# fp16 row sums for steps 13 and 14, their low parts' place on VectorE, and a different wait ahead of the experts' first layers

## The chip, the cores and the metric

The kernel runs on one core of one Trainium2 chip. The metric is the device time of one execution in microseconds (us). The engines are named as in the profile: PE (TensorE, matmuls), DVE (VectorE), ACT (ScalarE), POOL (GpSimd), SP (the queue that issues most DMAs).

## What is computed

Two batches of 512 tokens of width 128 and a context of 154 rows per batch. Layer normalisation, cross attention with 16 heads of width 64, a residual, layer normalisation again, and a mixture of 8 experts of which each token takes its best 2, with a residual:

```python
lat = layer_norm(_layernorm(x), g_l, b_l)            # 512 queries
kv_input = concatenate([layer_norm(ctx, g_m, b_m), lat])   # 154 + 512 = 666 keys
dots = einsum('bhid,bhjd->bhij', q, k) * 64 ** -0.5
attn = softmax(dots)
x = x + (einsum('bhij,bhjd->bhid', attn, v) merged) @ Wout
probs = softmax(n @ Wg); top 2, scaled to sum 1      # n = _layernorm(x)
h = relu((n masked) @ W1[e] + b1[e]); y = h @ W2[e] + b2[e]
x = x + sum over e of y * score[e]
```

## The kernel before, in words

**Attention.** It runs in STEPS = 16 steps `s`; a step is one pair of heads of one batch. In a step the 666 keys come in KT = 6 tiles of 111. Per tile PE computes the scores of both heads, keys on partitions and queries along the row (`dots`, L448 to 472; the shift by the row maxima is one of its matmuls, L470), ACT takes the exponential into `probs` (`exponent`, L785 to 792), and POOL adds the tiles of probabilities up in `psum_acc[:, s % 2]`, five additions a step (`gather`, L1330 to 1344, semaphore `added`). Between the tiles PE makes the scores of the next step for the maxima (`lead_next`), which DVE reduces (`reduce_max`, `join_max`), PE turns (`turn_max`) and DVE spreads into `max_row` (`spread_max`, L1005); the next step's `dots` need it. At the end of a step PE multiplies the probabilities with V (`pv`, L474 to 486).

**The sum of a row.** The softmax denominator is the sum of psum_acc over its 111 partitions, made on PE with a matrix of ones (`total`, L488 to 501). Up to step 12 (`s < HALVED`, HALVED = STEPS - 3 = 13) psum_acc is first split into two fp16 parts: ACT makes `acc_hi` (`sum_high`, L798 to 802), DVE makes `acc_lo`, the difference (`sum_low`, L1018 to 1021), and PE multiplies both (L493). From step 13 on PE multiplies psum_acc itself in fp32 (L499). ACT copies the sum to `recips` (`copy_sum`, L804), DVE takes reciprocals in four pieces (`reciprocal`, L1023), and POOL multiplies the step's output with them (`normalise`, L1346 to 1350, semaphore `o_norm`). acc_hi and acc_lo exist once, psum_acc and recips twice.

**The order of work** is written out by hand, one queue for each engine, with semaphores between them. In step s, `total(s - 1)` is queued on PE ahead of the last tile of `pv` (SUM_AT = 5), for s = 14 ahead of the first. ACT has `sum_high(s - 1)` behind the exponentials of step s, DVE has `sum_low(s - 1)` behind that step's spread maxima, and the reciprocals of step s - 2 behind that. Step 14 makes no projections of a later step; PE multiplies the output of batch 0 with Wout instead (`out_project(0)`).

**From step 15 on.** The attention output of batch 0 becomes x1 (`x1_and_moments(0)`), is normalised (`rstd_x1(0)` on POOL, `norm_x1(0)` on DVE), turned on PE (`turn_x2(0)`) and split into a high and a low part (`split_x2(0)`, three instructions). DVE's queue there: x1, norm, reciprocals of step 12, split, reciprocals of step 13, the gate (`gate_start`, `gate_end`), reciprocals of step 14. POOL's queue: `rstd_x1(0)`, `normalise(12)`, three running sums of step 15, `normalise(13)`, two more, `w2_low(1)`, then the experts. PE's queue: `turn_x2(0)`, the six tiles of `dots(15)`, `logits(0)`, `total(14)`, the six of `pv(15)`, `layer_one(0)`, `turn_scores(0)`, `layer_one(1)`, `total(15)`, `bias_term(0)`, `layer_one(2)` and so on. SP writes the turned scores to memory and reads them back as broadcast rows (`spread`, one DMA for each expert).

**The experts.** g = 0 to 15 is batch times expert. `layer_one(g)` (L655 to 669) makes two halves of hidden values (c = 0, 1) in four PSUM banks `hid_ps[n % 4]`, n = 2g + c, so expert g overwrites the banks of g - 2. ACT makes relu and its high part; the low part of the first half is made by POOL (`low_first`), that of the second half by DVE (`low_second`, L1156) or, for g in ON_POOL (L55: 5 to 10, 13, 14), by POOL (L1324 to 1328). For g in ON_POOL, ACT writes the second relu to SBUF (`relu_second_ring`), so the high and the low part are read from there; otherwise relu stays in the bank. The wait of `layer_one` for c = 1 is `second_low(pe, g - 2)` (L288 to 293): the low part of g - 2 must be made. `layer_two(g)`, queued LAG = 2 experts later, multiplies with W2; `add_expert` on DVE weighs and adds, each needing its broadcast rows. For g >= SCALED = 13 the weight goes into the hidden values ahead of relu (`scale_hidden`, DVE).

Of the kernel before, what the change touches and what calls it, by code (L numbers as in the profile page):

```python
# [27 lines left out]
STEPS = PAIRS * B  # L28
# [17 lines left out]
VH = KT // 2  # L46
RC = 4
WB = 4
HALVED = STEPS - 3
SUM_AT = KT - 1  # L50
W1_AT = {2: 0, 3: 1, 8: 2, 9: 3, 10: 4, 11: 5, 12: 6, 13: 7}
W2_HI_AT = {11: (0,), 12: (1, 2), 13: (3, 4), 14: (5, 6, 7)}
# [2 lines left out]
ON_POOL = [5, 6, 7, 8, 9, 10, 13, 14]  # L55
# [29 lines left out]
def xattn_moe(nc, x, ctx_in, g_m, b_m, g_l, b_l, wq, wkv, wout, wg, w1, b1, w2, b2, out):  # L85
    with ExitStack() as stack:
# [168 lines left out]
        r1_done = sem("r1_done")  # L255
# [132 lines left out]
        def _(pe):  # L388
# [99 lines left out]
            def total(s, bank=pj):  # L488
                if s < HALVED:
                    pe.wait_ge(acc_lo_done, s + 1)  # L490
                    for part in (acc_hi, acc_lo):
                        for h in range(2):
                            mm = pe.matmul(bank[h * HD:(h + 1) * HD, :], ones_h[0:KP, :], part[0:KP, h, :],  # L493
                                           start=(part is acc_hi), stop=(part is acc_lo))
                    mm.then_inc(sum_ready, 1)
                    return
                pe.wait_ge(added, (KT - 1) * (s + 1))
                for h in range(2):
                    mm = pe.matmul(bank[h * HD:(h + 1) * HD, :], ones[0:KP, :], psum_acc[0:KP, s % 2, h, :],  # L499
                                   start=True, stop=True)  # L500
                mm.then_inc(sum_ready, 1)
# [76 lines left out]
            for s in range(STEPS - 1):  # L578
                made = s + 2 < STEPS
                ahead = 0 if s else 1  # L580
                for kt in range(ahead):
                    dots(s, kt)
                for kt in range(ahead, KT):
                    dots(s, kt)
                    lead_next(s + 1, kt - ahead)
                if ahead:
                    lead_next(s + 1, KT - 1)
                if made:
                    pe.wait_ge(exp_done, s * KT + KT - 1)
                    if batch_of(s + 2) == 0:  # L590
                        pe.wait_ge(wqk_split, pair_of(s + 2))
                    elif s == 2:
                        pe.wait_ge(kv_lo_pool, 3)
                    project_q(s + 2)
                    project_k(s + 2, 0, sc[:, 0, 1, :])
                    pe.wait_ge(exp_done, s * KT + KT)
                    project_k(s + 2, 1, sc[:, 1, 0, :])
                else:
                    pe.wait_ge(tail_loaded, 16 * 4)
                    pe.wait_ge(max_done, (s + 2) * UNITS - 1)  # L600
                    pe.wait_ge(o_norm, STEPS - 4)
                    out_project(0, x1_ps[0], range(PAIRS))
                if v_half(s):
                    if v_weights(v_half(s)[0]) > 0:
                        pe.wait_ge(wv_split, v_weights(v_half(s)[0]))
                    pe.wait_ge(max_done, (s + 2) * UNITS - 1)
                    project_v(*v_half(s))
                pe.wait_ge(exp_done, s * KT + KT)
                if s == 1:
                    pe.wait_ge(max_done, (s + 2) * UNITS)  # L610
                    for n in range(QT):
                        mm = turn_inputs(1, n, pj[:, n * P:(n + 1) * P])
                    mm.then_inc(norm_turned, 1)
                    for n in range(QT, QT + CT):
                        at = P + (n - QT) * CP
                        mm = turn_inputs(1, n, sc[:, 1, 1, at:at + CP])
                    mm.then_inc(norm_turned, 1)
                turn_max(s + 1)
                if s > HALVED:
                    total(s - 1)  # L620
                for kt in range(KT):
                    if kt == SUM_AT and 1 <= s <= HALVED:
                        if s == 1:
                            pe.wait_ge(kv_ready, 3)
                        total(s - 1)
                    pv(s, kt)
# [28 lines left out]
            def layer_one(g):  # L655
                b, e = g // E, g % E
                if e == 0:
                    pe.wait_ge(x2_lo, b + 1)
                pe.wait_ge(w1_split, min(g + 1, E))
                for c in range(HC):  # L660
                    n = g * HC + c
                    if n < 4:
                        pe.wait_ge(exp_done, STEPS * KT - (1 if n < 2 else 0))
                    elif c == 0:
                        pe.wait_ge(r0_done, g - 1)
                    else:
                        second_low(pe, g - 2)
                    three(hid_ps[:, n % 4, :], w1_hi[:, e, c * P:(c + 1) * P], w1_lo[:, e, c * P:(c + 1) * P],
                          kv_hi[:, b, 0:N], kv_lo[:, b, 0:N]).then_inc(hid_ready, 1)
# [52 lines left out]
            s = STEPS - 1  # L722
# [41 lines left out]
        def _(act):  # L764
# [56 lines left out]
            g = E * HC  # L821
# [31 lines left out]
            def w2_high(e):  # L853
                act.wait_ge(tail_loaded, 16 * 4)
                act.wait_ge(k_lo_done, 2 * (STEPS - WB + e // 2 + 1))
                act.copy(w2_hi(e), w2_raw[:, e * HC:(e + 1) * HC, :]).then_inc(w2_hi_ready, 1)

            for s in range(STEPS):
                if s >= 1:
                    copy_output(s - 1)  # L860
                for kt in range(KT):
                    exponent(s, kt)
                if s + 2 < STEPS:
                    q_high(s + 2)
                    k_high(s + 2, 0, sc[:, 0, 1, :])
                    k_high(s + 2, 1, sc[:, 1, 0, :])
                if 2 <= s <= HALVED:
                    sum_high(s - 1)
                if v_half(s):
                    copy_v(*v_half(s))  # L870
                if s == 1:
                    second_inputs()
                    sum_high(s - 1)
                    second_high()
                if s >= 1:
                    copy_sum(s - 1)
                if s + 1 in W1_AT:
                    w1_high(W1_AT[s + 1])
                for e in W2_HI_AT.get(s, ()):
                    w2_high(e)  # L880

            def gate_exp_of(b):
                act.wait_ge(gate_sub, b + 1)
# [68 lines left out]
        def _(dve):  # L952
# [27 lines left out]
            def k_low(n, half, bank):  # L980
                dve.wait_ge(k_hi_done, 2 * n + half + 1)
                at = k_cols(half)
                dve.tensor_tensor(k_pair[:, n % QKB, 1, at], bank[:, 0:k_width(half)],
                                  k_pair[:, n % QKB, 0, at].bitcast(F32), ALU.subtract).then_inc(k_lo_done, 1)
# [20 lines left out]
            def spread_max(n, bank=sc[:, 1, 1, :]):  # L1005
                dve.wait_ge(neg_turned, n + 1)
                dve.tensor_tensor(max_row[:, n % 2, :].rearrange("p (t c) -> p t c", t=QT),  # L1007
                                  bank[:, 0:P].unsqueeze(1).to_broadcast([P, QT, P]),
                                  sel[:, :].unsqueeze(2).to_broadcast([P, QT, P]), ALU.mult).then_inc(row_done, 1)
# [8 lines left out]
            def sum_low(s):  # L1018
                dve.wait_ge(acc_hi_done, s + 1)
                dve.tensor_tensor(acc_lo[0:KP, :, :], psum_acc[0:KP, s % 2, :, :], acc_hi[0:KP, :, :],  # L1020
                                  ALU.subtract).then_inc(acc_lo_done, 1)
# [27 lines left out]
            g = E * HC  # L1049
# [33 lines left out]
            for s in range(STEPS - 1):  # L1083
                made = s + 2 < STEPS
                for u in range(UNITS):
                    reduce_max(s + 1, u)
                join_max(s + 1)
                if made:
                    q_low(s + 2)
                    k_low(s + 2, 0, sc[:, 0, 1, :])  # L1090
                spread_max(s + 1)
                if made:
                    k_low(s + 2, 1, sc[:, 1, 0, :])
                if s == 0:
                    second_moments()
                if 1 <= s <= HALVED:
                    sum_low(s - 1)
                if 2 <= s <= HALVED:
                    for c in range(RC):
                        reciprocal(s - 2, c)  # L1100

# [9 lines left out]
            def norm_x1(b):  # L1111
                dve.wait_ge(rstd_ready, RSTDS + b + 1)
                apply_norm(b, [(t, acc[:, b, t, :]) for t in range(QT)])
# [80 lines left out]

            x1_and_moments(0, x1_ps[0])
            norm_x1(0)
            for c in range(RC):
                reciprocal(STEPS - 4, c)
            split_x2(0)
# [230 lines left out]
```

## Time and profile before

| | us |
|---|---|
| median of 3 runs (341.89 to 341.97) | 341.89 |
| the profiled execution | 342.18 |
| its span | 340.2 |
| busy in it: PE, DVE, ACT, POOL | 331.9, 272.7, 214.8, 290.3 |
| the granted TensorE clock | full in all 40 slices |

The span runs from the first to the last instruction of the trace; the time around it is 2.0 us. An engine's busy time is an average over the whole: PE is busy nearly always, POOL nearly always during attention. What a part is worth is read from the timeline around it. Times of the timeline are counted from the span's start: attention's steps run from about 20 us at 15.8 us each, step 14 begins at 241 us, step 15 at 262 us, the experts at 276 us.

### The profile page before, as it was taken

What the parts mean: (1) busy time and instruction counts of PE and PEld (TensorE: products, weight loads), DVE (VectorE), ACT (ScalarE), POOL (GpSimd) and SP (SyncE); (2) the same over time, 40 slices, a digit from 0 to 9 for tenths busy, and PEclk for the clock granted to TensorE, in tenths of its full rate; (3) what the DMA queues carried; (4) which work ended last, traced back from release to release, by engine and by line L of the source; (5) the groups of instructions that cost most, each with busy time, mean ns of one, the idle gap of its engine ahead of it and who ended that gap; (6) DMA issues with size and microseconds to landing.
All of it is one profiled execution on the core that took longest, in us unless ns stands there. A gap on an engine that the chain in (4) does not pass through costs nothing.

```text
span 340.2 us, 6018 instructions
## 1 busy us (share of the span) xinstructions
PE 331.9 (98%) x2209; PEld 221.8 (65%) x2209; DVE 272.7 (80%) x413; ACT 214.8 (63%) x305; POOL 290.3 (85%) x188
## 2 busy tenths in 40 slices
PE   7899999999999999999999999999999999999986
PEld 7666666575747565665657584756594548888766
DVE  5989566988989899999898797979737797399494
ACT  2565678584949475675858494957622746487954
POOL 4639999999999999999999999899994899488543
PEclk9999999999999999999999999999999999999999
DMA  4640000000010000000000000000000006100520
GB/s 128 183 129 0 2 0 4 0 17 0 2 31 10 23 2 0 3 1 2 15 2 15 18 0 17 0 2 1 2 0 3 0 0 198 53 2 0 175 106 33
DMA packets 9049, 10.03 MB, mean 29 GB/s; under 512 B 1015, under 2 KB 6061, under 8 KB 9021
## 3 DMA queue, kind: packets, MB, share of 16 engines
q1 hardware_dynamic: 8725, 9.52, 9.0%
q8 instruction: 18, 0.29, 0.3%
q10 hardware_dynamic: 296, 0.13, 0.1%
q14 instruction: 10, 0.08, 0.1%
HBM read 9.09 MB, written 0.56 MB: 28 GB/s over the span
## 4 chain that ended last, share of the span: by engine, by line
PE 93%; issue 2%; ACT 2%; POOL 1%; DVE 1%; POOLq 0%; ACTq 0%; DVEq 0%
PE xo L484 25%; PE sc L464 21%; PE sc L470 6%; PE sc L390 5%; PE sc L391 4%; PE sc L392 4%; PE mx L421 3%; PE xo L421 3%; PE mx L572 2%; PE xo L572 2%; PE xo L493 2%; PE sc L505 2%; PE mx L391 1%; PE mx L390 1%; PE mx L392 1%
## 5 line engine op out<-in xcount | busy, mean ns | idle before, releaser
L1343 POOL TENSOR_TENSOR psum_acc<-psum_acc,probs 111x1024 f32<-111x1024 f32 x64 | 164.0, 2563 | 6.9
L792 ACT ACTIVATE probs<-sc 111x1024 f32<-111x1024 f32 x96 | 98.3, 1028 | 18.5 <-PE sc L470 11.3
L484 PE MATMUL xo<-probs,v_sb 111*64 111x512 f32 x384 | 88.0, 596 | 0.0
L464 PE MATMUL sc<-q_pair,k_pair 64*111 64x512 f32 x576 | 85.9, 401 | 0.8 <-ACT v_sb L782 0.4
L464 PEld LDWEIGHTS sc<-q_pair,k_pair 64*111 64x111 f32 x576 | 44.7, 170 | 28.3 <-issue 11.5
L484 PEld LDWEIGHTS xo<-probs,v_sb 111*64 111x64 f32 x384 | 26.3, 137 | 42.7 <-issue 39.4
L1026 DVE RECIPROCAL recips<-recips 128x128 f32<-128x128 f32 x64 | 54.0, 904 | 0.0
L992 DVE TENSOR_REDUCE part_max<-mx 128x2 f32<-128x888 f32 x32 | 34.7, 1084 | 21.0 <-PE mx L421 19.5
L808 ACT COPY recips<-xo 128x512 f32<-128x512 f32 x16 | 9.4, 587 | 57.5 <-PE xo L493 48.8
L1343 POOL TENSOR_TENSOR psum_acc<-probs 111x1024 f32<-111x1024 f32 x16 | 39.3, 2458 | 7.1 <-ACT probs L792 6.9
L470 PE MATMUL sc<-max_row,ones_r 64*111 64x512 f32 x192 | 38.3, 391 | 0.0
L1321 POOL TENSOR_TENSOR relu_lo<-relu_ring,relu_hi 128x512 fp32r<-128x512 f32 x16 | 20.7, 1291 | 15.7 <-ACT relu_hi L906 14.3
L992 DVE TENSOR_REDUCE part_max<-xo 128x2 f32<-128x888 f32 x30 | 32.5, 1084 | 1.7 <-PE xo L421 0.3
L1350 POOL TENSOR_TENSOR o_t<-o_t,recips 128x512 f32<-128x512 f32 x16 | 20.7, 1294 | 5.2 <-DVE recips L1026 5.2
L1020 DVE TENSOR_TENSOR acc_lo<-psum_acc,acc_hi 111x1024 f16<-111x1024 f32 x13 | 24.0, 1847 | 1.2 <-ACT acc_hi L802 1.2
L470 PEld LDWEIGHTS sc<-max_row,ones_r 64*111 64x111 f32 x192 | 17.0, 170 | 5.3
L421 PE MATMUL mx<-k_pair,q_pair 64*128 64x444 f32 (+1 forms) x128 | 18.2, 318 | 0.6 <-ACT k_pair L777 0.5
L996 DVE TENSOR_REDUCE part_max<-mx 128x4 f32<-128x888 f32 x16 | 17.3, 1082 | 1.4
L796 ACT COPY o_t<-xo 128x512 f32<-128x512 f32 x16 | 9.4, 588 | 13.8 <-PE xo L484 13.8
L1007 DVE TENSOR_TENSOR max_row<-sc,sel 128x512 fp32r<-128x512 f32 x15 | 10.4, 692 | 9.7 <-PE sc L445 9.6
L421 PE MATMUL xo<-k_pair,q_pair 64*128 64x444 f32 (+1 forms) x120 | 17.0, 316 | 0.0
L996 DVE TENSOR_REDUCE part_max<-xo 128x4 f32<-128x888 f32 x15 | 16.2, 1082 | 0.9
(241 smaller groups left out, 618.2 us busy)
## 6 DMA issues: line engine op xcount, KB each, us to landing
spread<-score_rows SPq DMA_DIRECT2D x16, 256.0 KB, 5.3
w_raw<-in_L_ffn_W SPq DMA_DIRECT2D x8, 128.0 KB, 2.1
x_tok<-in_x SPq DMA_DIRECT2D x2, 256.0 KB, 3.1
wv_raw<-in_L_xattn_Wkv SPq DMA_DIRECT2D x4, 128.0 KB, 3.4
wout_sb<-in_L_xattn_Wout SPq DMA_DIRECT2D x1, 512.0 KB
wqk_raw<-in_L_xattn_Wq SPq DMA_DIRECT2D x7, 64.0 KB, 1.9
wqk_raw<-in_L_xattn_Wkv SPq DMA_DIRECT2D x7, 64.0 KB, 2.3
out<-x_tok SPq DMA_DIRECT2D x1, 256.0 KB, 2.0
```

The source lines that it names most:

```text
L421: mm = pe.matmul(to, q_pair[r, n % QKB, 0, t * P:(t + 1) * P], k_pair[r, n % QKB, 0, k_cols(u >= QT)], start=True, stop=True)
L464: pe.matmul(sc[0:KP, kt % 2, h, :], k_pair[r, s % QKB, k_part, at], q_pair[r, s % QKB, q_part, :], start=(k_part + q_part == 0), stop=False)
L470: mm = pe.matmul(sc[0:KP, kt % 2, h, :], ones_r[r, :], max_row[r, s % 2, :], start=False, stop=True)
L484: mm = pe.matmul(o_ps[h * HD:(h + 1) * HD, :], v_sb[0:KP, s // 2 % 2, kt, at:at + HD], probs[0:KP, e % RING, h, :], start=(kt == 0), stop= ...
L792: act.activation(probs[0:KP, e % RING, :, :], sc[0:KP, kt % 2, :, :], ACT.Exp).then_inc(exp_done, 1)
L992: dve.tensor_reduce(part_max[:, 0, :, u], banks[:, :, 0:KW], AX.X, ALU.max, negate=True) \
L996: dve.tensor_reduce(part_max[:, 1, :, t:t + 2], banks[:, :, 0:2 * KR].rearrange("p h (t m) -> p h t m", m=KR), AX.X, ALU.max, negate=True) ...
L1020: dve.tensor_tensor(acc_lo[0:KP, :, :], psum_acc[0:KP, s % 2, :, :], acc_hi[0:KP, :, :], ALU.subtract).then_inc(acc_lo_done, 1)
L1026: dve.reciprocal(at, at).then_inc(recip_done, 1)
L1321: pool.tensor_tensor(relu_lo[:, g * HC % FR, :], relu_ring[:, g % 2, :], relu_hi[:, g * HC % FR, :].bitcast(F32), ALU.subtract).then_inc(l ...
L1343: pool.tensor_tensor(psum_acc[0:KP, s % 2, :, :], first, probs[0:KP, e % RING, :, :], ALU.add) \
L1350: pool.tensor_tensor(o, o, recips[:, s % 2, :], ALU.mult).then_inc(o_norm, 1)
```

## The change

Five edits go together.

1. HALVED becomes 15: sums 13 and 14 are made in fp16 from acc_hi and acc_lo; only sum 15 stays fp32. POOL's first running sum of step 15 waits for acc_lo of step 13 instead of its sum. Sum 13 keeps its place on PE, ahead of step 14's `pv`; sum 14 has its own call, ahead of step 15's `pv`, as before.
2. ACT: `sum_high(13)` behind step 14's exponentials, `sum_high(14)` as the last of step 14.
3. DVE, step 14: `sum_low(13)` ahead of `spread_max(15)`.
4. DVE, step 15: `sum_low(14)` behind `norm_x1(0)` and ahead of the reciprocals of step 12.
5. PE, `layer_one`, c = 1: where the low part of g - 2 is made by POOL, the wait is for its relu (`r1_done`) alone.

The reciprocals stay where they were (`s < STEPS - 2` is the same as `s <= 13`).

```diff
@@ -46,7 +46,7 @@
 VH = KT // 2
 RC = 4
 WB = 4
-HALVED = STEPS - 3
+HALVED = STEPS - 1
 SUM_AT = KT - 1
 W1_AT = {2: 0, 3: 1, 8: 2, 9: 3, 10: 4, 11: 5, 12: 6, 13: 7}
 W2_HI_AT = {11: (0,), 12: (1, 2), 13: (3, 4), 14: (5, 6, 7)}
@@ -616,10 +616,8 @@
                         mm = turn_inputs(1, n, sc[:, 1, 1, at:at + CP])
                     mm.then_inc(norm_turned, 1)
                 turn_max(s + 1)
-                if s > HALVED:
-                    total(s - 1)
                 for kt in range(KT):
-                    if kt == SUM_AT and 1 <= s <= HALVED:
+                    if kt == (SUM_AT if s < STEPS - 2 else 0) and s >= 1:
                         if s == 1:
                             pe.wait_ge(kv_ready, 3)
                         total(s - 1)
@@ -663,6 +661,8 @@
                         pe.wait_ge(exp_done, STEPS * KT - (1 if n < 2 else 0))
                     elif c == 0:
                         pe.wait_ge(r0_done, g - 1)
+                    elif g - 2 in ON_POOL:
+                        pe.wait_ge(r1_done, g - 1)
                     else:
                         second_low(pe, g - 2)
                     three(hid_ps[:, n % 4, :], w1_hi[:, e, c * P:(c + 1) * P], w1_lo[:, e, c * P:(c + 1) * P],
@@ -864,7 +864,7 @@
                     q_high(s + 2)
                     k_high(s + 2, 0, sc[:, 0, 1, :])
                     k_high(s + 2, 1, sc[:, 1, 0, :])
-                if 2 <= s <= HALVED:
+                if 2 <= s < STEPS - 1:
                     sum_high(s - 1)
                 if v_half(s):
                     copy_v(*v_half(s))
@@ -878,6 +878,8 @@
                     w1_high(W1_AT[s + 1])
                 for e in W2_HI_AT.get(s, ()):
                     w2_high(e)
+                if s == STEPS - 2:
+                    sum_high(s)
 
             def gate_exp_of(b):
                 act.wait_ge(gate_sub, b + 1)
@@ -1088,14 +1090,16 @@
                 if made:
                     q_low(s + 2)
                     k_low(s + 2, 0, sc[:, 0, 1, :])
+                else:
+                    sum_low(s - 1)
                 spread_max(s + 1)
                 if made:
                     k_low(s + 2, 1, sc[:, 1, 0, :])
                 if s == 0:
                     second_moments()
-                if 1 <= s <= HALVED:
+                if s >= 1 and made:
                     sum_low(s - 1)
-                if 2 <= s <= HALVED:
+                if 2 <= s < STEPS - 2:
                     for c in range(RC):
                         reciprocal(s - 2, c)
 
@@ -1194,6 +1198,7 @@
 
             x1_and_moments(0, x1_ps[0])
             norm_x1(0)
+            sum_low(STEPS - 2)
             for c in range(RC):
                 reciprocal(STEPS - 4, c)
             split_x2(0)
```

## Rows read from the trace of the kernel before

**Rows 1.** The page: busy us, share of the span, instructions, of each engine.

```profile
PE 331.9 (98%) x2209; PEld 221.8 (65%) x2209; DVE 272.7 (80%) x413; ACT 214.8 (63%) x305; POOL 290.3 (85%) x188
```

**Rows 2.** Who waited for whom, PE: us in total, times, longest.

```profile
PE sc L390 <- POOL relu_lo L1327: 1.3, 1, 1.3
```

**Rows 3.** The chain of waits: start us, us, what; the sums 12, 13, 14.

```profile
240.15 0.43 PE xo L493 x4
...
256.03 1.01 PE xo L499 x4
...
270.44 1.01 PE xo L499 x4
```

**Rows 4.** Lines L1020, L1343: duration ns min/median/max, first and last start.

```profile
L1020 DVE TENSOR_TENSOR acc_lo<-psum_acc,acc_hi x13: 1215/1769/2760, 48.7 to 236.6; 111x1024 f16<-111x1024 f32 x13
...
L1343 POOL TENSOR_TENSOR psum_acc<-psum_acc,probs x64: 2348/2404/3378, 25.8 to 277.1; 111x1024 f32<-111x1024 f32 x64
```

**Rows 5.** Timeline, step 13: start, us, engine line, instruction, idle before.

```profile
234.95 1.06 ACT L802 CAST acc_hi<-psum_acc 111x1024 f16<-111x1024 f32 x1
...
236.64 1.22 DVE L1020 TENSOR_TENSOR acc_lo<-psum_acc,acc_hi 111x1024 f16<-111x1024 f32 x1
...
237.78 3.38 DVE L1026 RECIPROCAL recips<-recips 128x128 f32<-128x128 f32 x4
```

**Rows 6.** Timeline, end of step 14 on DVE, POOL and ACT.

```profile
256.06 0.69 DVE L1007 TENSOR_TENSOR max_row<-sc,sel 128x512 fp32r<-128x512 f32 x1 [6.23 <-PE sc L445]
...
258.96 1.03 POOL L1378 TENSOR_TENSOR rstd<-var_eps,half_power 128x4 f32<-128x4 f32 x1 [1.13 <-DVE var_eps L1108]
...
262.23 0.59 ACT L796 COPY o_t<-xo 128x512 f32<-128x512 f32 x1 [3.65 <-PE xo L484]
```

**Rows 7.** Timeline, step 15: DVE, and PE's logits.

```profile
261.05 3.38 DVE L1026 RECIPROCAL recips<-recips 128x128 f32<-128x128 f32 x4
...
265.62 0.68 DVE L1120 COPY kv_t<-mx 128x512 f32<-128x512 f32 x1
...
269.39 1.06 PE L639 MATMUL mx<-wg_sb,kv_t 128*128 128x8 f32 x8
...
270.48 0.19 DVE L1124 TENSOR_REDUCE g_neg<-mx 128x4 f32<-128x32 f32 x1 [0.89 <-PE mx L639]
...
276.35 0.19 DVE L1153 TENSOR_TENSOR score<-mx,g_trec 128x32 f32<-128x32 f32 x1
```

**Rows 8.** Timeline, step 15: the exponentials (ACT) and POOL's queue.

```profile
263.93 1.96 ACT L792 ACTIVATE probs<-sc 111x1024 f32<-111x1024 f32 x2 [1.11 <-PE sc L470]
...
264.58 1.28 POOL L1350 TENSOR_TENSOR o_t<-o_t,recips 128x512 f32<-128x512 f32 x1 [4.59 <-DVE recips L1026]
...
265.97 2.45 POOL L1343 TENSOR_TENSOR psum_acc<-probs 111x1024 f32<-111x1024 f32 x1
...
274.64 4.91 POOL L1343 TENSOR_TENSOR psum_acc<-psum_acc,probs 111x1024 f32<-111x1024 f32 x2
```

**Rows 9.** Timeline, PE at sum 15.

```profile
279.64 0.39 PE L392 MATMUL sc<-kv_hi,w_lo 128*128 128x512 f32 x1
...
279.96 1.08 PE L499 MATMUL xo<-psum_acc,ones 111*64 111x512 f32 x4
```

**Rows 10.** Timeline at 320 us, and DVE's busy us in a window behind it.

```profile
320.18 0.70 DVE L1181 TENSOR_TENSOR xo<-xo,spread 128x512 f32<-128x512 f32 x1 [4.13 <-DMA spread<-score_rows]
...
320.18:332.90 12.72, 12.42 (x19) 1.00 0.42 146
```

**Rows 11.** Timeline, the wait in front of expert 15's second half.

```profile
329.65 1.27 POOL L1327 TENSOR_TENSOR relu_lo<-psum_acc,relu_hi 128x512 fp32r<-128x512 f32 x1
...
331.06 0.47 PE L390 MATMUL sc<-kv_hi,w_hi 128*128 128x512 f32 x1 [1.26 <-POOL relu_lo L1327]
```

**Rows 12.** Timeline, last expert: DVE's low part, and PE's use of it.

```profile
334.75 0.69 DVE L1162 TENSOR_TENSOR relu_lo<-sc,relu_hi 128x512 fp32r<-128x512 f32 x1 [0.17 <-ACT relu_hi L921]
...
335.56 0.39 PE L697 MATMUL mx<-relu_lo,wqk_lo 128*128 128x256 f32 x2
```

## The prediction

> **What bounds the kernel now.** I read the page first. TensorE (PE) is busy for 331.9 of the span's 340.2 us [rows 1], so the time is PE's queue plus the places where that queue stands still. The list of PE's waits has one of any size after the prologue: 1.3 us for GpSimd's relu_lo, once [rows 2]. The chain of waits prices the row sums: four passes in fp16 take 0.43 us (sum 12), in fp32 1.01 us (13 and 14) [rows 3]. From these three views alone the change looks like a gain: two sums become cheaper and a wait goes. So the work is in the engines that feed PE between step 14 and the experts: GpSimd (POOL), which does the running sums, and VectorE (DVE), which does the reciprocals. I went through the timelines of both from 230 us to the end.
>
> **Sums 13 and 14 on PE.** Each falls from 1.01 to 0.43 us, so PE gains 2 x 0.58 = 1.16 us, if nothing makes it wait. Both keep their place: `total(13)` ahead of step 14's products, `total(14)` ahead of step 15's.
>
> **What each now needs.** ScalarE (ACT) makes acc_hi (1.06 us), DVE makes acc_lo (1.22 us when nothing is in its way, and its next instruction starts 1.14 us after it) [rows 5].
> - Sum 13. `sum_high(13)` is queued on ACT behind step 14's last exponential, `sum_low(13)` on DVE behind `join_max` and ahead of `spread_max(15)`. DVE stands idle there for 6.23 us until PE's turned maxima arrive [rows 6], and 1.06 + at most 2.76 us (the longest acc_lo [rows 4]) fits in. So `spread_max(15)` and `total(13)` are not late: cost nothing on DVE, ACT and PE. If that cover were gone, the whole 1.06 + 1.22 us would stand ahead of step 15's first scores.
> - What sum_low(13) does cost is on POOL. Of POOL's running sums the median is 2.40 us and the longest 3.38 us [rows 4]; the long ones are those beside an acc_lo, so one sum is stretched by up to 0.98 us. Step 14's last running sum then ends that much later. Behind it comes `rstd_x1(0)`, before which POOL now idles for 1.13 us until DVE's var_eps [rows 6]. That row also gives the running sum's end, 258.96 - 1.13 = 257.83, in the new order 258.81. 0.98 fits in 1.13: I take nothing for it, with 0.15 us to spare. Here is the slower rival's door.
> - Sum 14. `sum_high(14)` on ACT waits for step 14's last running sum, 258.81, and ends at 259.9, ahead of sum_low(14)'s turn on DVE. Queued behind it is `copy_output(14)`, before which ACT idles for 3.65 us until 262.23 [rows 6] (261.65 in the new order, with PE 0.58 us ahead). Hidden. If this cover were gone, step 15's exponentials would be late by up to 1.06 us.
>
> **The instruction that is not hidden: sum_low(14).** It stands on DVE behind `norm_x1(0)` and ahead of the reciprocals of step 12, which now run from 261.05 [rows 7]. They start 1.14 us later. Who waits for them: POOL's `normalise(12)`, which even now idles 4.59 us for exactly these [rows 8]. Behind it in POOL's queue stand the five running sums of step 15, and the last of these ends at 274.64 + 4.91 = 279.55 [rows 8]; PE's `total(15)` waits for that one. All of it is back to back. There is one small reserve: the first of the five started when the exponential was done (second of a pair from 263.93, done about 265.89), at 265.97, while `normalise(12)` had ended at 264.58 + 1.28 = 265.86, and POOL's records otherwise overlap a little where nothing is waited for: some 0.15 us of waiting for the exponential. The exponentials are 0.58 us earlier now, so POOL's queue decides: the start moves by 1.14 - 0.15, 0.98 us by the unrounded figures, and the last running sum ends at 280.53.
>
> **PE meets it.** Before, PE issued its last matmul ahead of `total(15)` at 279.64 (they are issued 0.23 us apart, so it was free at 279.87) and started the sum at 279.96 [rows 9]: the 0.3 us between the running sum's end and PE shows that the two were already neck and neck. Now PE is there 1.16 us sooner, at 278.7, and the data come at 280.53. With 0.11 us for the semaphore, `total(15)` starts at 280.65: 1.9 us of new stall, and 280.65 - 279.96 = **0.69 us later than before**. The 1.16 us are swallowed whole; even if fp16 saved nothing, this number would be the same. The bounds of this term: 0 delay on POOL (then 279.55 - 0.15 + 0.11 = 279.51, a gain of 0.45), and 1.22 instead of 1.14 and no reserve (+0.92).
>
> **The other things that sum_low(14) is put in front of.** `split_x2(0)` moves by 1.14, its last copy from 265.62 + 0.68 to 267.4; the logits that read it begin at 269.39 - 0.58 = 268.8 [rows 7]: hidden, 1.4 us to spare. The reciprocals of step 13 end near 270.7, the gate's first operation was at 270.48 [rows 7], so up to 0.3 us there; but its exponential then no longer stands behind `copy_sum(14)`, which is 1.16 us earlier. The scores are finished at 276.54 [rows 7], PE takes them four transposes and six matmuls ahead of 279.87, at about 278.0, in the new order at 276.9: hidden. SP's queue: the DMA that writes the first scores waits for the last running sum as well, so it and the broadcast rows behind it can move by what total(15) moves, no more.
>
> **From total(15) to 320 us** PE's list of waits has nothing, from POOL, DVE or a DMA [rows 2], so its queue carries the 0.69 us on, and the scores of batch 1, their DMA and the broadcast rows move with it.
>
> **The removed wait.** With expert g - 2 in ON_POOL, the second hidden half of expert g needs relu's result only, not POOL's low part. It matters where PE really waited: expert 15, 1.26 us until POOL's relu_lo of 329.65 + 1.27 ended [rows 11]. The relu that it now waits for is what ACT casts and POOL reads before that, so it was long done, and PE is 1.26 us ahead. But what ends last there is not PE: from the broadcast rows at 320.18, after 4.13 us of idling for that DMA, DVE is busy 12.42 of 12.72 us [rows 10], with products, additions and the scaling of experts 13, 14 and 15 one behind the other. The scaling of 15 is the last of them and ends at 332.90, when DVE's queue gets to it; its first half needs nothing of what PE was held from. From it follow ACT's relu and cast and DVE's last low part, 334.75 + 0.69 = 335.44 [rows 12]; PE reads it in the second of the pair of matmuls that starts at 335.56, so at 335.68. Available at 335.55: only 0.13 us was PE's own. The removed wait gives **0.12 us** (from 0 to 1.26).
>
> **Sum.** +0.69 - 0.12 = +0.57 us on the profiled execution (342.18 us, span 340.2); the median of the runs is 341.89, 0.29 less. Forecast: 341.89 + 0.57 = 342.46, call it 342.5. Steps 1 to 13 are unchanged.
>
> **The skill, weighed.** The longest running sum is 0.98 us over the median where an acc_lo of 1.22 us lies beside it [rows 4]. The Trainium skill, "SBUF — State Buffer", section "SBUF: two separate sides", says that VectorE with two SBUF inputs and a GpSimd instruction that reads SBUF exclude each other for a whole instruction. By that rule the stretch would be the full 1.22 us; here that would exceed the 1.13 us of idling and add 0.09 us to the result. The row shows less, and I go by the row.
>
> **Rivals** (0.2%, or 0.68 us, is about what a measurement of this kernel tells from no change; it separates the classes below).
> - *POOL's cover breaks* (slower). sum_low(13) meets two of POOL's instructions, say two running sums (2 x 0.98 = 1.96), and `rstd_x1(0)` is late by 1.96 - 1.13 = 0.83. That hangs in series: norm, sum_low(14), reciprocals, running sums, total(15). It decides from 1.13 us of stretch on, and gives 342.46 + 0.2 to 0.83 = 342.7 to 343.3. For it: the acc_lo's durations reach 2.76 us, so the engines do meet in more than one way [rows 4]. Against: the longest single stretch is below the cover. 17%.
> - *The tail gives the wait back* (no loss). If DVE's row of work from 320 to 333 us is in truth paced by PE, the 1.26 us count in full: 0.69 - 1.26 = -0.57, 341.3. Against: PE's result for each of its parts was there before DVE took it. 9%.
> - *The reciprocals have slack* (faster). If POOL does not move, total(15) is 0.45 us earlier, with the tail 0.57: 341.3. If POOL gains what PE gains, 1.16 + 0.12 = 1.28: 340.6. Against: the 4.59 us for which POOL waits for just these. 6% and 3%.
> - *The forecast's case*, 342.1 to 342.8: 65%. This straddles the bound of +0.68 (342.57), and I give 38 of the 65 to the side within it.
>
> **Chances.** Faster by over 0.2%: the 3, and 4 of the two cases at 341.3 (9 + 6), which lie just inside the bound of 341.21: 7%. Within: 38 of the forecast's, 11 of those two, 2 of the late POOL's: 51%. Slower: 27 + 15: 42%. The range 341.3 to 343.2 leaves out the fastest case and the far end of the late POOL. The likeliest case's own range, 342.1 to 342.8, has the +0.92 as its upper bound; its lower takes 0.3 us for a tail that gives back more than 0.12.
>
> **What the changed profile would show.** The row sums of steps 13 and 14 at 0.43 us in the chain; DVE with acc_lo at about 250.5 and at 261.05, its next reciprocals at 262.2; POOL idling some 5.7 us until those, its last running sum ending near 280.5; PE waiting for it, a row of about 1.9 us in the list of waits, that was not there; the row L390 <- POOL relu_lo gone from it, and the last low part of DVE still followed by PE within 0.25 us. I am wrong if rstd begins later than 259.0, if total(15) starts before 280, or if the tail from the broadcast rows' landing to the end shrinks by over 0.3 us.

## The result, and the profile after

The changed kernel takes 344.1 us (median of 8 runs, 343.01 to 345.02), the kernel before 342.1 (8 runs, 341.89 to 342.93): 1.0052 times as long, 95% interval 1.0032 to 1.0072, so 1.1 to 2.5 us slower. The forecast was 342.46 and at most 343.2, slower by 0.57 us; the sign is right, the size is a third of what came. The profiled execution took 344.9 us. The page of the changed kernel: its span, PE's line of part 1, and the granted TensorE clock in 40 slices.

```profile
span 343.0 us, 6017 instructions
...
PE 333.1 (97%) x2209; PEld 222.8 (65%) x2209; DVE 277.4 (81%) x415; ACT 216.7 (63%) x307; POOL 290.8 (85%) x188
...
PEclk9999999999999999999999999999999998999999
```

PE is busy for 1.2 us longer than before although two of its sums are cheaper, and one slice of the clock is not full. Before, all were. Now the list of PE's waits (in total, times, longest):

```profile
PE xo L499 <- POOL psum_acc L1348: 1.6, 1, 1.6
...
PE mx L697 <- POOL relu_lo L1332: 0.5, 1, 0.5
```

The first is the new pause in front of sum 15, the second what is left of the wait of [rows 2]. The chain of waits (start, us, what) from step 14 to sum 15:

```profile
249.21 7.38 PE mx L572 x64
...
257.38 0.61 DVE x_tok L1108
258.02 0.88 DVE stats L964 x4
259.58 1.04 POOL rstd L1383
260.65 1.11 DVE normed L973 x4
261.76 1.14 DVE acc_lo L1022
262.90 3.31 DVE recips L1028 x4
266.34 1.29 POOL o_t L1355
267.63 2.41 POOL psum_acc L1348
...
278.78 2.38 POOL psum_acc L1348
281.29 1.08 PE xo L499 x4
```

Where PE's own matmuls filled this stretch before, the chain now leaves PE at `out_project(0)` and comes back only at sum 15: acc_lo, reciprocals, product, five running sums, as the prediction has it. Two traces are best laid side by side from a matmul that lies ahead of all edits, the first of `out_project(0)`: 248.58 before, 249.21 here. These 0.63 us come from the start of the kernel (see start_order). The marks in the timeline of the kernel before are its first `out_project(0)`, its first `out_project(1)` and DVE's last instruction, which stands for the end:

```profile
248.58 7.38 PE L572 MATMUL mx<-wout_sb,o_t 128*128 128x128 f32 x64
...
284.90 6.41 PE L572 MATMUL xo<-wout_sb,o_t 128*128 128x128 f32 x56
...
337.60 0.42 DVE L1192 TENSOR_TENSOR x_tok<-xo,x_tok 128x256 f32<-128x256 f32 x1 [0.18 <-PE xo L717]
```

The same in the changed kernel, with PE's last matmul ahead of sum 15 as the second row:

```profile
249.21 7.38 PE L572 MATMUL mx<-wout_sb,o_t 128*128 128x128 f32 x64
...
279.30 0.39 PE L392 MATMUL sc<-kv_hi,w_lo 128*128 128x512 f32 x1
...
287.80 6.41 PE L572 MATMUL xo<-wout_sb,o_t 128*128 128x128 f32 x56
...
340.43 0.42 DVE L1196 TENSOR_TENSOR x_tok<-xo,x_tok 128x256 f32<-128x256 f32 x1 [0.19 <-PE xo L717]
```

From the first of these marks on:

| us later than before, counted from out_project(0) | sum 15 | out_project(1) | DVE's last low part | last transpose | end |
|---|---|---|---|---|---|
| changed kernel | +0.70 | +2.27 | +2.27 | +2.20 | +2.20 |

So there are three steps: +0.70 until sum 15, +1.57 between sum 15 and out_project(1), and -0.07 at the end. The second is not in the prediction. The windows of the changed kernel around it (PE, PEld, DVE, ACT, POOL busy us with counts, PEclk, DMA share, GB/s):

```profile
279.60:281.30 1.70, 0.10 (x3) 0.04 (x2) 0.69 (x1) 1.67 (x4) 1.70 (x2) 1.00 0.00 0
281.30:282.00 0.70, 0.70 (x4) 0.19 (x4) 0.00 (x0) 0.70 (x2) 0.70 (x2) 1.00 0.00 0
282.00:283.00 1.00, 1.00 (x4) 0.29 (x2) 0.32 (x1) 0.97 (x3) 1.00 (x1) 1.00 0.09 16
283.00:284.00 1.00, 1.00 (x3) 0.55 (x3) 1.00 (x2) 0.68 (x2) 1.00 (x2) 0.81 0.16 57
284.00:285.00 1.00, 1.00 (x3) 0.73 (x3) 1.00 (x3) 0.13 (x2) 1.00 (x3) 0.50 0.62 178
285.00:286.00 1.00, 1.00 (x4) 0.78 (x3) 1.00 (x3) 0.97 (x2) 1.00 (x1) 0.50 1.02 348
286.00:287.00 1.00, 1.00 (x4) 0.81 (x3) 0.66 (x1) 0.97 (x3) 1.00 (x3) 0.50 0.99 344
287.00:288.00 1.00, 1.00 (x6) 0.82 (x6) 0.54 (x1) 0.43 (x1) 1.00 (x1) 0.99 1.01 193
```

Behind the pause (0.10 us busy of 1.70) PE works two microseconds at 2.4 GHz, then the granted clock is 0.50, which is 1.2 GHz, for over three microseconds, and 1.00 again. Its matmuls in the timeline stand 0.43 us apart there:

```profile
283.74 0.63 PE L391 MATMUL sc<-kv_lo,w_hi 128*128 128x512 f32 x1
284.17 0.63 PE L392 MATMUL sc<-kv_hi,w_lo 128*128 128x512 f32 x1
284.60 0.63 PE L390 MATMUL sc<-kv_hi,w_hi 128*128 128x512 f32 x1
```

In the kernel before, at 2.4 GHz, the same matmuls stand 0.23 us apart:

```profile
282.36 0.39 PE L391 MATMUL sc<-kv_lo,w_hi 128*128 128x512 f32 x1
282.59 0.39 PE L392 MATMUL sc<-kv_hi,w_lo 128*128 128x512 f32 x1
```

That is 0.20 us more for each, and nine such steps, the first and the last only partly slow, make up the 1.57 us. PE is "busy" all the while: only the clock column shows it. The Trainium skill, "TensorE: Matmul & The Clock Gate", section "What's actually happening", says that a gate halves the array's clock when PE has been too little busy; by that rule a pause can have a second price behind it. The trace agrees with the two levels, 1.00 and 0.50; what counts as too little no run here measures.

The clock did not fall in every run. Of the 8 runs, 5 have a mean clock of 0.993 and lie at 343.97 to 345.02, three have 0.998 to 1.00 and lie at 343.01 to 343.29.

Last, step 14 on DVE and POOL in the changed kernel's timeline (rows of before: [rows 4], [rows 6]):

```profile
248.07 8.18 POOL L1348 TENSOR_TENSOR psum_acc<-psum_acc,probs 111x1024 f32<-111x1024 f32 x3
...
250.95 3.09 DVE L1022 TENSOR_TENSOR acc_lo<-psum_acc,acc_hi 111x1024 f16<-111x1024 f32 x1 [0.48 <-ACT acc_hi L802]
...
259.58 1.03 POOL L1383 TENSOR_TENSOR rstd<-var_eps,half_power 128x4 f32<-128x4 f32 x1 [0.32 <-DVE var_eps L1112]
```

The three running sums took 7.38 us before and 8.18 now, a stretch of 0.80, and POOL's idle time ahead of rstd shrank from 1.13 to 0.32 us. The cover held.

### The profile page after: what moved, and what is told of

It is laid out like the page before. It is cut to its first block, busy times and chain, and to the rows that moved or that the text cites. A ratio compares the mean times of both kernels' runs of the same rounds, so it can differ in the third digit from the quotient of the medians.

```text
span 343.0 us, 6017 instructions
## 1 busy us (share of the span) xinstructions
PE 333.1 (97%) x2209; PEld 222.8 (65%) x2209; DVE 277.4 (81%) x415; ACT 216.7 (63%) x307; POOL 290.8 (85%) x188
## 4 chain that ended last, share of the span: by engine, by line
PE 85%; POOL 6%; DVE 3%; issue 3%; ACT 2%; POOLq 0%; ACTq 0%; DVEq 0%
PE xo L484 22%; PE sc L464 20%; PE sc L470 6%; PE sc L390 5%; PE sc L392 4%; PE sc L391 4%; POOL psum_acc L1348 3%; PE mx L421 3%; PE xo L421 3%; PE mx L572 2%; PE xo L572 2%; PE xo L493 2%; PE sc L505 2%; PE mx L390 1%; PE mx L391 1%
## 5 line engine op out<-in xcount | busy, mean ns | idle before, releaser
L1022 DVE TENSOR_TENSOR acc_lo<-psum_acc,acc_hi 111x1024 f16<-111x1024 f32 x15 | 28.6, 1908 | 1.7 <-ACT acc_hi L802 1.7
L390 PE MATMUL sc<-kv_hi,wqk_hi 128*128 128x222 f32 (+2 forms) x43 | 16.2, 377 | 0.3 <-ACT v_sb L782 0.3
```

Source lines behind the costliest of these rows:

```text
L390: pe.matmul(out_ap, st_hi, mv_hi, start=True, stop=False)
```

## The experiments

All times are against the kernel before on the same chip, whose median was 342.27 us (35 runs) for filler, only13, low_late and wait_alone, 341.90 (24 runs) for dve_delay, double_low, norm_late and start_order, and 342.11 (23 runs) for best13 and start_other. The edits of wait_alone and dve_delay are shown against the kernel before, those of start_order and start_other against only13, the others against the changed kernel. "Frame" is the table's way of counting, from `out_project(0)`, on the one profiled execution of each kernel; "the end" is the start of DVE's last instruction.

**filler: PE's pause filled**

```diff
                 if g == 1:
+                    for _ in range(5):
+                        pe.matmul(mx[:, 0, 0:P], ident[:, :], ident[:, :], start=True, stop=True)
                     pe.wait_ge(o_copied, STEPS)
                     total(s, o_ps)
```

> The changed kernel, with five fp32 128x128 matmuls into an unused bank on PE in front of sum 15, where PE stands still for 1.6 us (they took some 0.24 us each in the prologue, together about 1.2 us). Theory (the idle stretch lets the granted clock fall, and the half clock of 283.3 to 287 us costs 1.57 us): the granted clock is 1.00 throughout in all or nearly all runs, the matmuls behind sum 15 are 0.23 us apart and not 0.43, and the time is 1.0 to 1.6 us below the changed kernel's median, about 342.9, still 0.6 to 0.9 above before. Rival (the clock falls for a reason that has nothing to do with PE's pause, such as the broadcast DMAs that start at the same time): the mean clock stays at 0.993 in most runs and the time stays near 344.

342.51 us (12 runs), ratio 1.0011 (1.0001 to 1.0022). The clock was 0.999 or 1.00 in all 12 runs. In the frame sum 15 is 0.73 later, out_project(1) 0.73, the end 0.66: the +1.57 is gone and the +0.70 stands. The sum in its timeline, with a pause of 0.45 left:

```profile
280.45 1.08 PE L499 MATMUL xo<-psum_acc,ones 111*64 111x512 f32 x4 [0.45 <-POOL psum_acc L1350]
```

The broadcast DMAs run as before, so they alone don't make the clock fall; with most of PE's idle stretch filled it did not fall in any run.

**only13: sum 14 stays fp32**

```diff
-HALVED = STEPS - 1
+HALVED = STEPS - 2
...
-                if s == STEPS - 2:
-                    sum_high(s)
...
-            sum_low(STEPS - 2)
```

> The changed kernel with sum 14 left in fp32 as before (no acc_hi and acc_lo of step 14); sum 13 in fp16 and the new wait of the first layers stay. Theory (all of the loss comes from the low part of step 14, which stands ahead of the reciprocals of step 12): POOL's last running sum ends where it did or 0.1 earlier, sum 15 starts 0.4 to 0.5 us earlier than before (PE arrives 0.58 us earlier, the running sum allows 0.45), the pause is under 0.3 us, the clock stays at 1.00, and the time is 0.3 to 0.6 us under before: about 341.5. Rival (sum 13's acc_lo, which took 3.09 us and stretched POOL's sums by 0.8 us, is what delays the chain): sum 15 no earlier than before, time at or above before.

341.41 us (12 runs), ratio 0.9983 (0.9973 to 0.9994): a little faster than before. Frame: sum 15 at -0.42, the end at -0.50. The clock was 1.00 at sum 15; the mean of 0.998 in three runs is, in the profiled one, a fall in the last 1.5 us, behind PE's last matmuls. Its acc_lo of step 13 took 3.04 us and stretched POOL's sums like the changed kernel's, and nothing was late for it. Sum 13 in fp16 pays; sum 14 is what costs.

**low_late: sum 14's low part behind the reciprocals**

```diff
-            sum_low(STEPS - 2)
             for c in range(RC):
                 reciprocal(STEPS - 4, c)
+            sum_low(STEPS - 2)
```

> The changed kernel with the low part of sum 14 moved behind the reciprocals of step 12 on DVE. Theory A (only DVE's order matters): the product of POOL that waits for these reciprocals starts 1.1 us earlier, sum 15 starts 0.4 to 0.5 us earlier than before, no clock drop, about 341.4. Theory B (an acc_lo also holds POOL up by about a microsecond wherever POOL runs beside it, as it stretched the running sums by 0.8 to 1.0 us): the low part now meets POOL's product of step 12, which takes 2.3 in place of 1.28 us, the last running sum ends as late as in the changed kernel within 0.3 us, and the time stays at 343 to 344.

342.89 us (12 runs), ratio 1.0018 (1.0003 to 1.0033); sum 15 at +0.34 in the frame, the clock at 0.993 to 0.995 in 5 of 12. Neither theory alone: the order gives back its 1.14 us, and a part is lost again to the meeting of the two engines:

```profile
264.17 1.16 DVE L1022 TENSOR_TENSOR acc_lo<-psum_acc,acc_hi 111x1024 f16<-111x1024 f32 x1
...
264.39 2.08 POOL L1355 TENSOR_TENSOR o_t<-o_t,recips 128x512 f32<-128x512 f32 x1 [4.59 <-DVE recips L1028]
```

POOL's product takes 2.08 in place of 1.28 us [rows 8]. It ends at 266.47, 1.14 us behind the end of DVE's instruction (265.33), as if it had stood almost until DVE was done. So POOL's queue paid 0.80 us in both places where it worked beside a new acc_lo, here and in step 14; where the change put sum 14's, POOL was idle but DVE was on the path.

**wait_alone: the new wait on the kernel before**

```diff
                         pe.wait_ge(r0_done, g - 1)
+                    elif g - 2 in ON_POOL:
+                        pe.wait_ge(r1_done, g - 1)
                     else:
```

> The kernel before with only the new wait of the first layers. My step (the tail is paced by DVE, PE's own share is 0.12 us): the 1.26 us wait is gone from PE's list, the end comes 0.05 to 0.15 us earlier, ratio 0.9996, not to be told from 1. Rival (the wait counts in full): 1.2 us faster, ratio 0.9965.

341.84 us (12 runs), ratio 0.9991 (0.9981 to 1.0). Frame: zero until DVE's last low part, the last transpose at -0.06, the end at -0.07. The 1.3 us wait became this one:

```profile
PE mx L699 <- POOL relu_lo L1329: 0.5, 1, 0.5
```

**dve_delay: the kernel before with an unused DVE instruction of acc_lo's shape**

```diff
             norm_x1(0)
+            dve.tensor_tensor(acc_lo[0:KP, :, :], psum_acc[0:KP, 0, :, :], acc_hi[0:KP, :, :], ALU.subtract)
             for c in range(RC):
```

> The kernel before (all three last sums in fp32, the old wait), with one more DVE instruction of acc_lo's shape (1.22 us) between norm_x1(0) and the reciprocals of step 12; its result is not used. Theory (the path runs DVE, reciprocals, POOL's product, five running sums, sum 15): POOL's product starts 1.1 us later, the last running sum 1.0 later, PE pauses 0.7 to 0.8 us at sum 15, which starts 0.65 to 0.7 us later; if the clock stays up, the time is 0.6 to 0.7 above before (ratio 1.002). If a pause of this length is enough for the clock to fall, some executions show 0.993 and lie 1.5 us higher still. Rival (the fp16 sums or ACT's acc_hi carry the loss): no change from before.

343.24 us (7 runs), ratio 1.004 (1.0026 to 1.0054); 2 of 7 runs with a clock of 0.995, at 344.09 and 344.18. Sum 15 at +0.74, the end at +0.76 in the frame of the profiled run, whose clock was 1.00. With neither sum 13 nor sum 14 in fp16 the path moves as in the changed kernel:

```profile
261.63 1.22 DVE L1197 TENSOR_TENSOR acc_lo<-psum_acc,acc_hi 111x1024 f16<-111x1024 f32 x1
...
266.30 1.29 POOL L1351 TENSOR_TENSOR o_t<-o_t,recips 128x512 f32<-128x512 f32 x1 [5.73 <-DVE recips L1026]
...
281.28 1.08 PE L499 MATMUL xo<-psum_acc,ones 111*64 111x512 f32 x4 [0.72 <-POOL psum_acc L1344]
```

**double_low: sum 14's low part made twice**

```diff
+            dve.wait_ge(acc_hi_done, STEPS - 1)
+            chained(dve.tensor_tensor(acc_lo[0:KP, :, :], psum_acc[0:KP, 0, :, :], acc_hi[0:KP, :, :], ALU.subtract))
             sum_low(STEPS - 2)
```

> The changed kernel with the low part of sum 14 made twice, one behind the other (1.2 us more on DVE at the same place). Theory: every piece of the path moves on by 1.15 to 1.25 us, PE's pause at sum 15 grows from 1.6 to some 2.8 us, the clock falls in more of the executions than the 6 in 8 of the changed kernel, if it is the pause that does it in all of them, and the time is about 345.2 (1.2 above the changed kernel's median of 344.1, 0.3 more if the clock falls every time). Rival (the fall is a matter of chance that does not depend on the pause): the same share of executions with the low clock.

346.85 us (4 runs), ratio 1.0144 (1.0129 to 1.016), 1.6 us more than the 345.2 expected. (The expectation puts the changed kernel's share of runs with a fall at 6 in 8; it is 5 in 8.) Sum 15 at +1.92, 1.22 beyond the changed kernel, as expected; but the clock fell in 4 of 4 runs (0.989 to 0.995) and in the profiled one stayed down about twice as long: out_project(1) is at +4.77 and DVE's last low part at +5.08, so the fall cost 2.85 us by the first and 3.16 in all, in place of 1.57. Its pause, and the clock in four of its windows of 2 us:

```profile
PE xo L499 <- POOL psum_acc L1350: 2.8, 1, 2.8
```

```profile
283.00:285.00 2.00, 2.00 (x7) 0.36 (x3) 1.14 (x2) 0.59 (x1) 2.00 (x2) 0.75 0.09 26
285.00:287.00 2.00, 2.00 (x6) 1.61 (x6) 2.00 (x4) 0.89 (x2) 2.00 (x3) 0.50 0.81 254
287.00:289.00 2.00, 2.00 (x7) 1.52 (x6) 0.55 (x1) 1.94 (x4) 1.92 (x3) 0.50 0.86 268
289.00:291.00 2.00, 2.00 (x9) 1.71 (x8) 1.23 (x2) 0.22 (x1) 2.00 (x3) 0.55 0.98 341
```

**norm_late: POOL's product of step 13 behind the last running sum**

```diff
             gather(STEPS - 1, 3)
-            normalise(STEPS - 3)
             gather(STEPS - 1, 4)
             gather(STEPS - 1, 5)
+            normalise(STEPS - 3)
```

> The changed kernel with POOL's product of step 13 (1.27 us) moved behind the last running sum of step 15. Theory (POOL's queue is what sum 15 waits for): the last running sum ends 1.24 us earlier than in the changed kernel, the pause falls to 0.4 to 0.7 us, sum 15 starts about 0.55 us earlier than before, the clock stays at 1.00, and the time is 0.5 to 0.7 under before, some 341.4. Rival (something else holds sum 15 or the experts behind it): 343 or more.

341.79 us (11 runs), ratio 0.9999 (0.999 to 1.0008), the clock at 1.00 in all 11. Sum 15 at -0.36 and the end at -0.44 in the frame, with a pause of 0.56. The cause holds: with POOL relieved, its frame ends 2.64 us ahead of the changed kernel's, in whose profiled execution the clock fell. I had expected 0.2 us more at sum 15; the runs show no gain over before that could be told from none, and the frame's 0.44 us is more than their interval allows (0.34 at most), which stays open.

**best13: only13 with the same move**

> The kernel with sum 14 in fp32, sum 13 in fp16 and the new wait, and POOL's product of step 13 moved behind the last running sum of step 15. Theory: the running sums end a microsecond before PE wants them, so sum 15 starts when PE gets there, 0.58 us earlier than before and 0.15 earlier than without the move (there it was 0.42 earlier); with the tail's 0.07 the time is 0.6 to 0.65 under before with the same start, ratio 0.998; the clock stays at 1.00. Rival (with the pause gone PE is held by another engine right away): 0.42 or less at sum 15, no gain over the kernel without the move.

341.68 us (12 runs), ratio 0.9982 (0.997 to 0.9994). Sum 15 at -0.51, the end at -0.59 in the frame, no pause, the clock never under 0.998. The frame puts it 0.09 us ahead of only13; by the runs the two are equal, and both beat the kernel before and the changed one.

**start_order and start_other: the start of the kernel.** Several kernels, before too, have two clusters of times some 0.9 us apart (before: about 341.6 to 342.3 and 342.5 to 343.2). The traces differ at 8.7 us, here before, then changed:

```profile
8.68 0.96 DVE L1056 TENSOR_TENSOR kv_lo<-kv_t,kv_hi 128x256 fp32r<-128x256 f32 x2
8.73 0.63 POOL L1260 CAST wqk_hi<-wqk_raw 128x256 fp32r<-128x256 f32 x1
```

```profile
8.67 0.40 POOL L1265 CAST wqk_hi<-wqk_raw 128x256 fp32r<-128x256 f32 x1
8.69 1.52 DVE L1058 TENSOR_TENSOR kv_lo<-kv_t,kv_hi 128x256 fp32r<-128x256 f32 x2
```

So it is in all ten traces with no wait added here: in four of them DVE begins first, its pair takes 0.96 to 1.10 us and `out_project(0)` starts at 248.34 to 248.58; in six the cast begins first, the pair takes 1.30 to 1.52 us and `out_project(0)` starts at 249.13 to 249.41. Both experiments add one wait to only13: in start_order POOL's cast waits for DVE's low part, in start_other DVE waits for the cast.

```diff
+                if p == 1:
+                    pool.wait_ge(kv_lo_ready, 2)
                 pool.tensor_copy(wqk_hi[:, p % WB, :, :], wqk_raw[:, p % 2, :, :]).then_inc(wqk_hi_ready, 1)
```

```diff
+            dve.wait_ge(wqk_hi_ready, 1)
             for i, at in enumerate(X_HALVES):
```

> The kernel with sum 14 in fp32 and sum 13 in fp16, with one more wait at the start: POOL's cast of the second pair's weights waits until DVE has made the low part of the first keys. Theory (the two groups of times of every kernel, 0.9 us apart, are decided at 8.7 us, where this cast and DVE's low part meet: whichever starts first holds up the other, 0.96 or 1.52 us for the low part): DVE's low part takes 0.96 us in every execution and the upper group is gone: all runs within 0.3 us. They lie at the lower group's 341.35, or up to 1 us higher if POOL's cast, 0.9 us later, is itself waited for. Rival (the groups come from elsewhere): both groups are still there.

> The kernel with sum 14 in fp32 and sum 13 in fp16, with one wait at the start in the other direction: DVE's low part of the first keys waits until POOL has made its cast. Theory (POOL's cast and the subtraction behind it, when they start first, hold DVE's low part up, and that makes the upper group of times): the low part takes 1.3 to 1.5 us, the first scores start at 12.0 to 12.2 us and not at 11.1 to 11.4, and nearly all runs lie in the upper group, 342.1 to 342.6. Rival (the order at this place and the group are only seen together): two groups as without the wait, most runs at 341.3 to 341.5.

start_order: 341.64 us (11 runs, 341.1 to 342.17), ratio 0.9986 (0.9976 to 0.9997). DVE's pair took 0.88 us. The gap between clusters is gone, but the runs spread evenly over 1.1 us and not over 0.3, up to just under only13's upper cluster (4 of 12 runs at 342.22 to 342.43, on another chip), so the expectation failed and something else varies too; that stays open. start_other: 342.99 us (12 runs, 342.24 to 344.9), ratio 1.0032 (1.0015 to 1.0049): no run lies where best13's lower cluster is on the same chip (341.15 to 341.70). Its pair took 1.29 us, and PE, which waits for it 1.1 us, has a mean clock of 0.99 to 0.995 in 5 of its 12 runs; in the profiled one the clock was low from about 12 to over 18 us. A window of that:

```profile
14.00:16.00 2.00, 2.00 (x9) 1.78 (x9) 1.02 (x2) 0.60 (x1) 1.84 (x4) 0.50 1.11 361
```

So the order at this place goes with the cluster in every trace, and DVE made to come second puts every run up; that it alone makes the clusters is not shown, since start_other's wait is a delay of its own. The clock can be low behind a pause elsewhere as well.

## Why the prediction was right and wrong, point by point

- *Sums 13 and 14, two times 0.58 us less on PE:* a little less. By the starts of its instructions PE's last matmul ahead of sum 15 comes 0.97 us sooner in the frame (279.64 - 248.58 against 279.30 - 249.21), not 1.16. As the prediction says, this size did not matter: all of it was swallowed by sum 15.
- *sum_low(13) hidden, at most 0.98 us on POOL inside 1.13:* right, 0.80 and 0.32 left. Its duration of 3.09 us was beyond the longest row I had (2.76), which had no effect. The rival "POOL's cover breaks" did not happen, in no trace.
- *sum_low(14) on the path, +1.14 us to the reciprocals, last running sum 0.98 later, sum 15 at +0.69:* right, +0.70; shown by only13 (taken away: -0.42, where I had put -0.45) and by dve_delay (put in alone: +0.74).
- *"PE's queue carries the 0.69 us on":* **this is the step that failed.** I priced the pause of 1.9 us (1.6 by the trace) as lateness alone, and so put the clock behind it at nothing. It has a second price: behind the pause the clock falls to half, which cost 1.57 us in the profiled execution. No rival had it, although the kernel itself has matmuls named `keep_awake` at its start. With the clock's fall in 5 of 8 runs, 0.63 (that is 0.70 - 0.07) + 5/8 x 1.57 = 1.6 us is expected of a mean run; the means of the runs differ by 1.8, the interval is 1.1 to 2.5. None of the prediction's own signs of being wrong came (in the time of the kernel before, rstd is at 258.95 and sum 15 at 280.66, and the tail from the first use of the broadcast rows is 0.07 us shorter): they watched the waits and not the clock.
- *The removed wait gives 0.12 us, not 1.26:* right in kind. It gave 0.06 to 0.07. One reading behind it was wrong: I took DVE's row of work from 320 us to be paced by the broadcast rows. In wait_alone and in filler DVE gets these rows 0.21 and 0.23 us later in the frame and its last low part comes no later than sum 15's shift. So its row of work had room for 0.2 us of lateness; that it is nearly full and ends last holds.
- *The running sums' stretch beside sum_low(13):* 0.80 us was measured, and the prediction's choice of the row over the page was right. By the lock of the Trainium skill, "SBUF — State Buffer", section "SBUF: two separate sides", it would have been 1.22 us. The rule's other half, that the one that starts first holds the other up, agrees with the rows of low_late (POOL's product 2.08 us) and of 8.7 us (DVE's pair 1.52 us).
- *The range:* it took in the start's two clusters and the +0.92, and had no term for the clock; that is why 344.1 lies outside.

How often the clock fell, by the pause at sum 15 in the profiled run. A run counts when its mean clock is at most 0.995; where in the run the clock fell is traced only for the profiled ones (changed kernel, low_late, double_low: behind sum 15):

| kernel | pause at sum 15, us | runs with a fall |
|---|---|---|
| only13, best13 | none listed | 0 of 24 |
| filler | 0.45 | 0 of 12 |
| norm_late | 0.56 | 0 of 11 |
| dve_delay | 0.72 | 2 of 7 |
| low_late | 1.25 | 5 of 12 |
| changed kernel | 1.60 | 5 of 8 |
| double_low | 2.82 | 4 of 4 |

That the pause is the cause is shown by filler, which takes the fall away, and borne out by double_low, where a longer pause brings it in every run. Why the same pause lets it fall in one run and not in another these runs don't show.

## What to carry to other kernels

Work moved off the busiest engine is worth only what its feeders leave: before making PE's part cheaper, look at who delivers next and how much it is ahead; here it was 0.3 us. And, in a kernel like this one, price a new pause of PE twice, as lateness and, from some 0.7 us on in this kernel, as a chance of a stretch at half clock behind it; independent matmuls in the pause took the second away (ratio to before 1.0052, then 1.0011), and not making the pause took both (0.9983). Where the order of two engines at one place differs from execution to execution, whole traces are shifted (here by 0.6 to 1.1 us); compare them from a mark behind the start.

## What the runs showed of the hardware that I had not expected

- A PE pause of 1.6 us was followed, two microseconds after its end, by over three at a granted clock of 0.50, which cost 1.57 us; behind one of 2.8 us the low clock cost 3.16 us. With pauses of 0.45 and 0.56 us no run of 12 and of 11 had a fall.
- A DVE subtraction of two SBUF tensors (1.22 us alone) took up to 3.09 us beside POOL's running sums, and POOL's product 2.08 in place of 1.28 when DVE had begun 0.22 us earlier. At the start of the kernel a pair of DVE instructions took 1.52 us when POOL's cast had begun 0.02 us earlier, and 0.96 when DVE had begun 0.05 us earlier.
